# Two mixture-of-experts layers on one core: a third tile buffer in layer 0, separate store counts, other numbers in the scheduling table

## The reference

```python
xn = layernorm(x)
x = x + attention(xn) + moe0(xn)      # causal softmax, 16 heads of 8; 16 experts of width 64, top 2, and a shared expert
xn = layernorm(x)
x = x + delta(xn) + moe1(xn)          # recurrence over the 256 tokens; 4 usable experts of width 704, top 2

def step(state, inp):                 # delta, per head: an 8x8 state
    kk = kt[..., :, None] * kt[..., None, :]
    state = state * (1.0 - bb * kk) + bb * (vt[..., :, None] * kt[..., None, :])
    out_t = einsum('bhij,bhj->bhi', state, qt)
```

## Time and profile before

| | |
|---|---|
| three runs | 2001.16 us median (1997.99 to 2007.99) |
| profiled execution | 2013.11 us, of which 2011.4 us are its span |
| busy | PE 1567.2, DVE 1395.0, ACT 978.3, POOL 905.1 us |
| granted TensorE clock | 0.865 of full speed |
| chain that ended last | PE 43%, DVE 15%, issue 14%, ACT 8%, POOL 6%, DMA 5%, SP's queue 4%, unknown 4% |

### The profile page before, as it was taken

How to read it: one execution, slowest core, us unless ns; L and a number is a source line. 1 busy time by engine, 2 the same in 40 slices (tenths; PEclk the granted TensorE clock), 3 DMA queues, 4 the chain that set the end, 5 groups by cost and what they waited for, 6 DMA issues and landing times.

```text
span 2011.4 us, 29786 instructions
## 1 busy us (share of the span) xinstructions
PE 1567.2 (78%) x9764; PEld 967.2 (48%) x9766; DVE 1395.0 (69%) x2664; ACT 978.3 (49%) x1600; POOL 905.1 (45%) x973
## 2 busy tenths in 40 slices
PE   2953977898777998888654887999999988698950
PEld 2840444454444554444332554656666655465530
DVE  5775655676555776776677855788888878787822
ACT  2721545565444665445444544556665644455410
POOL 4247437725543224658786265111111257621126
PEclk9875979998776999778776888999999989999985
DMA  6954678888655765656445374565665657665423
GB/s 207 291 150 140 197 196 232 246 224 225 193 163 169 207 176 139 160 151 191 114 130 183 111 214 151 162 187 172 172 185 170 185 181 230 200 179 167 131 80 90
DMA packets 277946, 354.44 MB, mean 176 GB/s; under 512 B 32272, under 2 KB 204304, under 8 KB 272416
## 3 DMA queue, kind: packets, MB, share of 16 engines
q1 hardware_dynamic: 237600, 287.92, 50.4%
q0 software_dynamic: 17056, 33.66, 5.8%
q10 hardware_dynamic: 23136, 30.94, 4.5%
HBM read 197.48 MB, written 122.68 MB: 159 GB/s over the span
## 4 chain that ended last, share of the span: by engine, by line
PE 43%; DVE 15%; issue 14%; ACT 8%; POOL 6%; DMA 5%; SPq 4%; another core or an unknown queue 4%; ACTq 0%; DVEq 0%; POOLq 0%
PE Y L1062 7%; PE R L819 5%; PE R L821 5%; PE R L820 5%; PE R L835 3%; POOL xs_dram L1368 3%; DVE state L2024 3%; PE Y L957 3%; PE R L922 2%; ACT probs L1535 2%; PE R L895 2%; DVE row_max L1923 2%; DVE acc_in L1749 2%; DVE dw L2018 2%
## 5 line engine op out<-in xcount | busy, mean ns | idle before, releaser
L1923 DVE TENSOR_REDUCE row_max<-R 128x6 f32<-128x768 f32 x256 | 241.3, 953 | 133.3 <-PE R L922 65.8
L1388 POOL TENSOR_TENSOR o_acc<-o_acc,read 128x512 f32<-128x512 f32 x112 | 143.9, 1284 | 408.4 <-DVE read L2034 407.5
L1368 POOL DMA_INDIRECT xs_dram<-sc_in,pos x256 | 269.4, 1052 | 109.5 <-issue 63.6
L1347 POOL DMA_INDIRECT gat<-ys_dram,pos x256 | 253.8, 992 | 133.2 <-issue 68.0
L1379 POOL TENSOR_SCALAR_AFFINE_SELECT probs<-probs 128x512 f32<-128x512 f32 x256 | 167.7, 655 | 316.6 <-ACT probs L1535 312.6
L1062 PE MATMUL Y<-hid,fd 128*128 128x512 f32 x456 | 250.0, 630 | 35.2 <-DVE hid L2072 26.5
L1535 ACT ACTIVATE probs<-R 128x768 f32<-128x768 f32 x256 | 205.0, 808 | 137.6 <-PE R L945 91.9
L819 PE MATMUL R<-fhl,fw 128*128 128x512 f32 x418 | 231.8, 555 | 19.2 <-issue 5.1
L2072 DVE TENSOR_TENSOR hid<-R,sil 128x512 f32<-128x512 f32 x228 | 155.7, 686 | 60.1 <-ACT sil L1654 24.4
L2024 DVE TENSOR_TENSOR_SCAN state<-dw 128x512 f32<-128x512 f32 x128 | 172.3, 1346 | 16.2 <-issue 7.9
L1654 ACT ACTIVATE sil<-R 128x512 f32<-128x512 f32 x190 | 112.9, 595 | 140.1 <-PE R L821 103.0
(11 more groups left out here) (270 smaller groups left out, 3479.7 us busy)
## 6 DMA issues: line engine op xcount, KB each, us to landing
fw<-wf SPq DMA_DIRECT2D x38, 1408.0 KB
q_rows<-kq SPq DMA_DIRECT2D x128, 256.0 KB
fx<-xs_dram SPq DMA_DIRECT2D x86, 256.0 KB
xs_dram<-gat SPq DMA_DIRECT2D x24, 512.0 KB, 4.6
qk_dram<-qk_parts SPq DMA_DIRECT2D x32, 384.0 KB
Q<-qk_dram SPq DMA_DIRECT2D x64, 192.0 KB
K<-qk_dram SPq DMA_DIRECT2D x64, 192.0 KB
fw<-wf SPq DMA_DIRECT2D x96, 128.0 KB
```

What stands on the lines that cost most here:

```text
L1347: pool.indirect_dma_start(gat[:, i % 2, 2 * t + a, :], None, ys_dram[l][g], bass.IndirectOffsetOnAxis(ap=pos[l][g][a][:, col:col + 1], axi ...
L1368: pool.indirect_dma_start(xs_dram[g], bass.IndirectOffsetOnAxis(ap=pos[l][g][a][:, col:col + 1], axis=0), sc_in[:, n % 2, t * P:(t + 1) * ...
L1923: dve.tensor_reduce(row_max[:, b, h2, :, :], pair[:, :].rearrange("p (g c t) -> p g c t", g=2, t=P)[:, :, 0:3, :], AX.X, ALU.max).then_inc ...
```

## The change

1. Layer 0's expert tiles get three buffers (`F0_BUFS = 3`) for rows and weights, so that LF0 waits for FD0 three tiles back, and `fy0` gets two.
2. `c_saved` becomes three counts, `x1_saved`, `x1n_saved`, `xT1_saved`; each user waits for its own. C1 waits for the store of x1 alone, C1b for that of x1n, C2 and LD for that of xT1, LS for that of x1n, and LDx now waits for x1 itself.
3. In the table: `soon` 2.8 becomes 4.4, a scatter or gather costs 1.28 instead of 1.03, the load of a tile 2.7 instead of 2.0 with a landing of 8.0.
4. Target times: second scatter 164.2 and 8.4 a chunk; tiles of group 1 59 earlier than the row of tiles would give; W pieces from 178.2, 47.9 apart; attention halves 79.3 + 22j up to 27, then 18.7 apart; sums of layer 0 43 behind their chunk's attention instead of 17; first tile of layer 1 at 803.3 (attention's planned end less 9.4, where it was plus 15), then 13.3 apart; delta chunks still 40 apart and begun 60 before attention's planned end; layer 1 scatters 74 behind their sums instead of 32.

```diff
-    soon, later = 2.8, 6.0
+    soon, later = 4.4, 6.0
...
-        t = 240 + 45 * (n - 2)
+        t = 178.2 + 47.9 * (n - 2)
...
-                stage(t + every * i + every * k / 8, "SC", m, k, after=after, POOL=1.03)
-    tb = a_time(NCH - 1) + 20
-    fast = 18
+                stage(t + every * i + every * k / 8, "SC", m, k, after=after, POOL=1.28)
+    tb = a_time(NCH - 1) + 16.3
+    fast = 27
...
-    f0_start = a_time(7) + 50 + 8.5 * 8 + 8
-    f0 = [f0_start + 8.8 * f for f in range(sum(NT[0]))]
+    f0_start = a_time(7) + 126 - 4.5
+    f0 = [f0_start + 8.8 * f - 59.0 * (f >= NT[0][0]) for f in range(sum(NT[0]))]
...
-            after = since(f, 2, ("FD0", 0, "PE"))
+            after = since(f, F0_BUFS, ("FD0", 0, "PE"))
...
-            stage(t - 7, "LF0", f, after=after + [("RC4", 0, g, "DVE")], SP=2.0)
-            stage(t, "FT0", f, after=[(("LF0", f, 0, "SP"), soon + 1)], PE=0.55,
+            stage(t - 12, "LF0", f, after=after + [("RC4", 0, g, "DVE")], SP=2.7)
+            stage(t, "FT0", f, after=[(("LF0", f, 0, "SP"), 8.0)], PE=0.55,
...
-        c.append(max(hw(2 * n + 3.6) + 17, f0[sum(NT[0][:g + 1]) - 1] + 12, (c[-1] if c else 0) + 14))
+        c.append(max(hw(2 * n + 3.6) + 43.0, f0[sum(NT[0][:g + 1]) - 1] + 12, (c[-1] if c else 0) + 14))
...
-        t = max(b_end + 15, c_end[g] + 42 + 9 * CHUNKS[1][g], (f1[-1] if f1 else 0) + 16)
-        f1 += [t + 16 * f for f in range(NT[1][g])]
+        t = max(b_end - 9.4, c_end[g] + 147.8, (f1[-1] if f1 else 0) + 16)
+        f1 += [t + 13.3 * f for f in range(NT[1][g])]
...
-            t = max(f1[sum(NT[1][:g + 1]) - 1] + 32, d[n] + 56, t + 10)
+            t = max(f1[sum(NT[1][:g + 1]) - 1] + 65.0, d[n] + 56, t + 10)
...
-    route(0, 0, a_time(7) + 14)
-    scatter(0, 0, a_time(7) + 50, 8.5)
+    route(0, 0, a_time(7) + 22.1)
+    scatter(0, 0, a_time(7) + 69.7, 8.5)
...
-    scatter(0, 1, 240, 11)
+    scatter(0, 1, 164.2, 8.4)
...
-    scatter(1, 0, c_end[0] + 32, 9)
+    scatter(1, 0, c_end[0] + 74.0, 9.3)
...
-                    if n >= 2:
-                        sp.wait_ge(*bank_of["fy0", n - 2].filled())
-                    sp.dma_start(fx0[:, par, :, :].rearrange("p (s t) d -> p s (t d)", s=2),
+                    if n >= F0_BUFS:
+                        sp.wait_ge(*bank_of["fy0", n - F0_BUFS].filled())
+                    sp.dma_start(fx0[:, n % F0_BUFS, :, :].rearrange("p (s t) d -> p s (t d)", s=2),
...
-                    if n >= 1:
-                        act.wait_ge(*f0_saved(n - 1))
+                    if n >= 2:
+                        act.wait_ge(*f0_saved(n - 2))
...
-                        dve.wait_ge(*c_saved(n - 1))
+                        dve.wait_ge(*x1_saved(n - 1))
```

More of the change, by code:

```diff
@@ L83 @@
 XIN = 4
+F0_BUFS = 3
 class Plan:
@@ L271, in scatter @@
             m = l * NCH + n
-            saved = [(("SAx", n, 0, "SP"), soon)] if l == 0 else [(("C1b", n, 0, "ACT"), soon), (("SC1", n, 0, "SP"), soon)]
+            saved = [(("SAx", n, 0, "SP"), soon)] if l == 0 else [(("C1b", n, 0, "ACT"), soon)]
             stage(t + every * i - 4, "LS", l, n, after=saved + since(m, 2, ("SC", 2 * TILES - 1, "POOL"), lag=soon),
@@ L302, in experts0 @@
             stage(t + 2, "FD0", f, after=[("FU0", f, 0, "DVE")], PE=0.6,
-                  ACT=(1.05, since(f, 1, ("FD0", 0, "ACT"), lag=soon)))
+                  ACT=(1.05, since(f, 2, ("FD0", 0, "ACT"), lag=soon)))
             banks("FD0", f, 0, ("FD0", f, 0, "ACT"), 2)
@@ L381, in sums0 @@
                 after = [(("FD0", sum(NT[0][:g + 1]) - last, 0, "ACT"), soon) for last in (1, 2)] if k == 0 else []
-                stage(t + 1.2 * k, "CG", n, k, after=after + (free if k == 0 else [("CG", n, k - 1, "POOL")]), POOL=1.03)
+                stage(t + 1.2 * k, "CG", n, k, after=after + (free if k == 0 else [("CG", n, k - 1, "POOL")]), POOL=1.28)
             stage(t + 12, "C1", n, after=[(("CL", n, 0, "SP"), soon), (("CG", n, 2 * TILES - 1, "POOL"), soon)]
-                  + since(n, 1, ("C1b", 0, "ACT"), ("SC1", 0, "SP"), lag=soon), DVE=4.1, POOL=pow4)
+                  + since(n, 1, ("C1b", 0, "ACT"), lag=soon), DVE=4.1, POOL=pow4)
             stage(t + 16, "C1b", n, after=[("C1", n, 0, "POOL")], DVE=0.1, ACT=2.1)
-            stage(t + 18, "C2", n, after=[("C1b", n, 0, "ACT")], PE=0.55, ACT=(whole, since(n, 1, ("C3", 0, "PE"))), DVE=odd)
+            stage(t + 18, "C2", n, after=[("C1b", n, 0, "ACT")], PE=0.55,
+                  ACT=(whole, since(n, 1, ("C3", 0, "PE")) + since(n, 1, ("SC1", 0, "SP"), lag=later)), DVE=odd)
             banks("C2", n, 0, ("C2", n, 0, "DVE"))
@@ L434, in table @@
         t = c[n] + 34
-        d.append(max(t, d[-1] + 40) if d else max(t, b_end - 60))
+        d.append(max(t, d[-1] + 40.0) if d else max(t, b_end - 60))
     def delta():
         for n, t in enumerate(d):
-            after = [(("SC1", n, 0, "SP"), soon), (("C1b", n, 0, "ACT"), soon)] + since(n, 1, ("D0", 0, "PE"), ("D0b", 0, "PE"), ("D1g", 0, "PE"))
+            after = [(("SC1", n, 0, "SP"), later)] + since(n, 1, ("D0", 0, "PE"), ("D0b", 0, "PE"), ("D1g", 0, "PE"))
             if n == 0:
@@ L472, in delta @@
             banks("D1g", n, 0, ("D1g", n, 0, "DVE"))
-            stage(t + 35, "LDx", n, after=[("LD", n, 0, "SP")] + since(n, 1, ("SD", 0, "SP"), lag=soon), SP=issue)
+            stage(t + 35, "LDx", n, after=[(("C1b", n, 0, "ACT"), soon), ("LD", n, 0, "SP")] + since(n, 1, ("SD", 0, "SP"), lag=soon), SP=issue)
             stage(t + 40, "D3a", n, after=[("DS", n, HD - 1, "POOL")], PE=0.4, ACT=(whole, since(n, 1, ("D3d", 0, "DVE"))),
@@ L495, in sums1 @@
                 after = [(("FZ1", sum(NT[1][:g + 1]) - last, 0, "ACT"), soon) for last in (1, 2)] if k == 0 else []
-                stage(t + 1.1 * k, "EG", n, k, after=after + (free if k == 0 else [("EG", n, k - 1, "POOL")]), POOL=1.03)
+                stage(t + 1.1 * k, "EG", n, k, after=after + (free if k == 0 else [("EG", n, k - 1, "POOL")]), POOL=1.28)
             stage(t + 10, "E1", n, after=[(("EL", n, 0, "SP"), soon), (("EG", n, 2 * TILES - 1, "POOL"), soon)], DVE=2.4)
@@ L712, in two_layer_kernel @@
         x_acc = sb("x_acc", [P, C])
-        fx0 = sb("fx0", [P, 2, TILES, P])
+        fx0 = sb("fx0", [P, F0_BUFS, TILES, P])
         fT0 = sb("fT0", [P, 2, C])
         hid0 = sb("hid0", [P, 2, C])
-        fy0 = sb("fy0", [P, C])
-        fw0 = sb("fw0", [P, 2, 2, W0E])
+        fy0 = sb("fy0", [P, 2, C])
+        fw0 = sb("fw0", [P, F0_BUFS, 2, W0E])
         sb, top_w = region(after_qk)
@@ L888, in _ @@
                     bank = take("R", ("fT0", n))
-                    turn(bank, lambda t: fx0[:, par, t, :]).then_inc(bank.full, 1)
+                    turn(bank, lambda t: fx0[:, n % F0_BUFS, t, :]).then_inc(bank.full, 1)
                 if kind == "FU0":
@@ L894, in _ @@
                         to = slice(s * S, (s + 1) * S)
-                        ins = pe.matmul(bank[:, to], fw0[:, par, s, 0:2 * F0], fT0[:, par, to], start=True, stop=True)
+                        ins = pe.matmul(bank[:, to], fw0[:, n % F0_BUFS, s, 0:2 * F0], fT0[:, par, to], start=True, stop=True)
                     ins.then_inc(bank.full, 1)
@@ L902, in _ @@
                         to = bank[:, (t // 2) * C + (t % 2) * P:(t // 2) * C + (t % 2 + 1) * P]
-                        ins = pe.matmul(to, hid0[rows, par, t * P:(t + 1) * P], fw0[rows, par, t // 2, 2 * F0:W0E],
+                        ins = pe.matmul(to, hid0[rows, par, t * P:(t + 1) * P], fw0[rows, n % F0_BUFS, t // 2, 2 * F0:W0E],
                                         start=True, stop=True)
@@ L1519, in _ @@
                     act.dma_start(ys_dram[0][g][f * C:(f + 1) * C, :].rearrange("(s p t) d -> p s (t d)", s=2, t=2),
-                                  fy0[:, :].rearrange("p (s c) -> p s c", s=2)).then_inc(f0_saved.sem(n), 16)
+                                  fy0[:, par, :].rearrange("p (s c) -> p s c", s=2)).then_inc(f0_saved.sem(n), 16)
                 if kind == "BM":
```

32 lines of the change are left out of this document (17 added, 15 removed).

## The result

The changed kernel takes 1851.1 us (median of four runs, 1847.0 to 1860.8) against 2003.4 us before in the same session: a ratio of 0.925, 95% interval 0.920 to 0.929. The profiled execution took 1851.7 us, its span 1850.0.

What follows compares the result with a forecast made beforehand. No engine is full; the order on POOL and SP was taken to bound the kernel. Terms -15 - 5 - 35 + 20 - 5 + 4 - 7 = -43 us from 2001.2 gave 1958 us, range 1905 to 2025.

Steps and rivals of the forecast that it cites:

- Longer landings: Table's believed landings, 2.8 to 4.4 us: no gain of its own, it stands behind the fifth taken for SP.
- Third buffer: Layer 0 tile loads on SP: most of 77.7 us of waits go, a fifth counts, -15 us (0 to 40).
- Own counts: Chunk stores in layer 0: C1's 6.6 us wait for the transposed store goes, -5 us (0 to 10).
- Earlier experts of group 1: Layer 0's last tiles near 690 instead of 767, layer 1 begins sooner: -35 us (0 to 71).
- Second scatter: POOL, layer 0: about 40 scatters in a row hold up attention, +20 us (0 to +36).
- First scatter: POOL at the start: begun later and costed dearer, some 9 scatters fewer ahead of the first mask, -5 us.
- Layer 1: Joint stage and end: tiles 13.3 apart, -29 joint stage, +88 recurrence alone, -55 tail, sum +4 us (-16 to +26).
- Spread of layer 1's scatters: Second group's 48 scatters get later targets, behind more urgent steps: -7 us (0 to -16).
- W pieces: Their transfers move by 62 to 53, to a time with free DMA engines as before: nothing.
- the gaps close further: Rival: attention keeps TensorE at 92% also in 900:1090, half of SP's waits on the path; -113, typical 1915 us, chance 0.18.
- The slower one: Rival: on POOL the second scatter starves attention, 2016 to 2038, taken as 2030 us; chance 0.20.
- the clock's: Rival: TensorE's clock falls when the recurrence is alone, up to 29 us more, 1987 us; chance 0.10.

Runs made afterwards that it cites:

- L alone: The kernel before with only the table's new lags and lengths (soon 4.4, indirect transfers 1.28, tile load 2.7 landed after 8.0): ratio 0.964, 1944 us.
- T1 undone: The changed kernel with layer 1's old target times alone (first expert tile at attention's planned end plus 15, tiles 16 apart): ratio 0.947, 1901 us.
- T0: Layer 0's new target times; the changed kernel with the old ones (second scatter from 240, tiles not 59 earlier, W pieces from 240): ratio 0.952, 1913 us.

## Why the prediction was wrong

The direction and the shape of the end were right; the sum was 109 us short. The planner's own end fell by 51, near the 43 that were forecast; the other 100 us and more are the distance between plan and chip (296 to 185), which the prediction left as it was. By its steps:

**Longer landings: booked at nothing.** This is the step that failed most. I had the rows that the table contradicted (4.3 and 6.3 us against 2.8, 1.26 us for an indirect transfer and its gap against 1.03) and gave them no price, since no single wait of the trace names them. Alone they gave 3.6%, 73 us; undone together with the counts they cost 5.0%, 100 us. That they work through the order is shown, for the run of L alone changes only the table, and nothing comes out of the table but the order and the choice of banks.

What the runs don't settle is why 4.4 is good: 1.4 was no worse than 2.8, and 5.6 with 7.5 seems 1.3% worse than 4.4. The planner's ends fit a trade: with 1.4 the plan gets 31 shorter and the chip's time stays as it was, with 5.6 and 7.5 the plan gets 51 longer and the run some 24. That 4.4 is the measured landing is not shown. The traces of the sessions at 1942 and 1945 us name more landings of 256 KB on SP's queue than the earlier trace rows does, and their medians go from 2.1 us (attention's store) over 2.7 (a tile's rows) and 4.0 to 5.4 (x) to 7.1 (the recurrence's store). The section of the Trainium skill that the prediction cites (DMA: Bandwidth & Descriptors, "Anatomy of one DMA — SWDGE (gpsimd) path") gives 2.0 us and the bytes over 436 GB/s, an estimate of 2.6 us here; it states this for transfers issued by GpSimd, and these are SP's. Its 2.6 us is near the 2.7 of a tile's rows and far from the 4.3 and 6.3 of the earlier trace rows. It would have left the table as it was, and 4.4 alone gave 2.4%.

**Third buffer: 15 booked, 36 alone, 52 when undone.** The term was mis-sized by the fifth that I took. The waits did not mostly go: SP still has 48.4 us of them (77.7 before). Alone, the buffers removed 30 us of these waits and gave 36, so nearly all of what went had been on the path.

**Own counts: 5 booked, 23 when undone.** Which waits these are is open. The plan gets 30 longer with the single count, since whoever needs one store then waits for the transposed one in the table too, and the run lost as much as that to within 7 us.

**Earlier experts of group 1: 35 booked.** In the changed kernel the mechanism is there: the last load came at 613.7 (690 forecast), and the first layer 1 tile is loaded 3 us behind attention's last store. But it holds only in company. On the old table both sets of times together moved the first layer 1 load by less than 1 us; layer 0's moved it 14 us the wrong way beside the buffers, 38 us the right way beside the lags, and 79 us in the finished kernel. On the old lags the experts came 46 to 48 us earlier and attention's last store 23 to 25 us later, so what one gained the other lost. I priced this part as though the rest stood still.

**Second scatter: +20 booked, nothing came.** I read the target times as if they were the order. The planner takes a step only when it is ready, and 31 masks stood between the 64 scatters, in the plan as on the chip. A comparison of the two kernels' orders would have shown it; the prediction had none. **First scatter: 5 booked.** The 9 scatters fewer ahead of the first mask were right (36 for 45), but not for the later begin that I gave first: with new target times alone there are still 45, with an indirect transfer costed at 1.28 alone 37, and with all of L alone 20. The price was wrong too: attention's first store moved from 237.0 to 208.4, 29 us, and L moves it alone (218.2 in that trace).

**Layer 1: +4 booked, 22 gained.** The changed kernel against the one with T1 undone: joint stage 767 for 827 us, overhang 98, tail 10 for 71. So -60 + 98 - 61 = -23, where I had -29 + 88 - 55. Two of the three terms were right within 10 us. The joint stage was mis-sized: I took 2.2 chunks less in it, at the 13 us that a chunk needs of TensorE; it was three chunks less, and each was worth 20 us. VectorE is at 80 to 85% in that stage, which may be why; no run shows it. On the old lags the same sum is -48 + 106 - 61 = -3 (layer 1's times alone against before), and the run says +0.7% in all.

**Spread of layer 1's scatters: 7 booked.** No run undoes it by itself. With T1 undone the first tile load comes 16 us later, and the spread is at most a part of that. The W pieces, booked at nothing, moved with T0 and were not run apart either.

**Rivals.** The one that lies nearest is that the gaps close further, to 1888 by its full sum. Its reason came in part: in attention's last stretch TensorE went from 67% to 80%, past the 75% that I had booked and short of the rival's 92%. The slower one, scatters that starve attention, didn't happen. Of the clock's, the level was right: 0.60 in 1742:1840, at 35% work, and 0.50 in the last 10 us without any. The price was not. Each kind of matmul of 1742:1840 can be set against the same kind in 1300:1440, where 0.99 was granted: one takes 1100 ns instead of 592, another 539 instead of 508, and all of them together 13 us more. So at most 13 of the 29 us lie in it. The Trainium skill (TensorE: Matmul & The Clock Gate, "What's actually happening") has 1.2 GHz for an idle array and 2.4 for a busy one; the 0.50 without work and the 0.99 at 97% agree with that.

**What would show it.** Right: attention's last store before 1060 (at 972, far more than forecast) and the first layer 1 tile within 10 us of it, the gathers beside the recurrence, last expert store 98 us ahead of the last chunk (90 forecast), under 25 us to the end. Wrong: the run of 40 scatters with TensorE below 60%, the last load at 690, tile waits down to a few us (the longest is 6.5), the last two chunks 35 to 45 us apart (50 and 35).

## What to carry to other kernels

Where a table or a planner writes the order of in-order engines, put landings and lengths near the measured ones in first, and only then tune target times: new times on the old lags gave 1.2% here, and 3.1% on the new ones with the third buffer and the counts. Set the planner's own end beside the measured span: as long as the distance changes with what is put in, the plan can't price a part. A list of start times is no order; print the order itself before arguing from it. When parts interact like this, a sum over parts that each stand on the old trace can be off either way (layer 1's times alone lost 0.7%, the three numbers of the table gave less together than singly), and its range has to say so.

## What was not expected of the hardware

A third of the shorter span is not less idle time of TensorE but less busy time for the same matmuls: 1513.0 us instead of 1567.2, at a mean granted clock of 0.887 for 0.865 (by the ratio of the clocks alone it would be 39 of the 54 us). Stretches that hold TensorE up cost twice, by the idle time and by a lower clock for the work in them: in 120:200 before had 159 ns of busy time for each matmul at 0.60, after 107 at 0.68, though not of the same kinds throughout. And the session matters: the unchanged kernel took 1942 to 2017 us (medians) in different sessions, those behind the first each on another chip, more than most parts of this change are worth. Its granted clock was 0.873 to 0.888 in the two faster ones and 0.858 to 0.874 in the others.
